# First attention of a two-layer gated block: heads in two halves of the array, queries stacked in lots, a later zero fill and a new order of each pair of steps

## The reference, cut to what matters

```python
x = x + jnp.tanh(g_xattn[0]) * _L0_xattn_ref(_layernorm(x), ctx, Wq, bq, Wk, bk, Wv, bv, Wo, bo)

q = jnp.einsum('btd,hdk->bhtk', tgt, Wq) + bq[None, :, None, :]
k = jnp.einsum('bsd,hdk->bhsk', src, Wk) + bk[None, :, None, :]
v = jnp.einsum('bsd,hdk->bhsk', src, Wv) + bv[None, :, None, :]
weights = jax.nn.softmax(jnp.einsum('bhtk,bhsk->bhts', q, k) / sqrt(16), axis=-1)
out = jnp.einsum('bhts,bhsk->bhtk', weights, v)
return h @ Wo + bo          # h: the heads of out side by side
```

## Time and profile before

| | us |
|---|---|
| runs of the kernel before | 961.48, 964.19, 970.35 (median 964.19) |
| the profiled execution's own time | 963.44 |
| its span, from the first to the last instruction | 961.7 |
| TensorE busy over the span | 754.5 (78%) |
| VectorE busy | 619.2 (64%) |
| ScalarE busy | 481.3 (50%) |
| GpSimd busy | 410.3 (43%) |

### The profile page before, as it was taken

The page is one execution under the profiler, slowest core; times in us unless marked ns, Lnnn a source line. Parts: engine busy times, 40 slices in busy tenths (PEclk is TensorE's granted clock), DMA queues, the critical chain, the costliest instruction groups (busy, mean ns, idle before and its releaser), DMA issues. The chain is left out here.

```text
span 961.7 us, 20435 instructions
## 1 busy us (share of the span) xinstructions
PE 754.5 (78%) x6519; PEld 573.3 (60%) x6519; DVE 619.2 (64%) x1458; ACT 481.3 (50%) x989; POOL 410.3 (43%) x437
## 2 busy tenths in 40 slices
PE   4679999999977398979888889578777548998830
PEld 2356667667656398978666656467666526665420
DVE  8567677767664669873444444377788436666766
ACT  4736565556544467652333333245655236776632
POOL 4268323233160028881000000586856716746455
PEclk9779999999999669999999999788989868999985
DMA  6447322223170238753222221378532212323233
GB/s 159 114 103 164 92 61 67 56 64 77 30 243 9 90 88 274 236 186 114 72 66 67 68 70 48 103 192 206 162 107 67 63 53 91 115 72 96 83 90 100
DMA packets 84511, 101.50 MB, mean 106 GB/s; under 512 B 16518, under 2 KB 70758, under 8 KB 84422
## 3 DMA queue, kind: packets, MB, share of 16 engines
q1 hardware_dynamic: 69526, 68.42, 25.4%
q0 software_dynamic: 12960, 30.74, 11.4%
q10 hardware_dynamic: 1936, 1.17, 0.5%
HBM read 61.03 MB, written 24.38 MB: 89 GB/s over the span
## 5 line engine op out<-in xcount | busy, mean ns | idle before, releaser
L645 DVE TENSOR_REDUCE a_mx<-ps 112x2 f32<-112x750 f32 x128 | 119.8, 936 | 45.1 <-PE ps L323 38.7
L529 ACT ACTIVATE a_Pf<-ps 125x672 f32<-125x672 f32 x128 | 89.7, 729 | 15.6 <-PE ps L271 14.6
L323 PE MATMUL ps<-a_stkK,a_stkQ 96*112 96x375 bf16 x256 | 68.2, 349 | 20.8 <-DMA a_stkK<-a_KS 10.6
L51 PE MATMUL ps<-f_w2hi,f_hh 128*128 (+1 forms) x292 | 81.3, 278 | 3.1 <-DVE f_hl L1432 3.1
L1430 DVE CAST f_hh<-ps 128x512 bf16<-128x512 f32 x41 | 28.4, 692 | 83.9 <-PE ps L1171 83.9
L51 PE MATMUL ps<-f_w2lo,f_hh 128*128 (+1 forms) x292 | 81.2, 278 | 0.0
L51 PE MATMUL ps<-f_w2hi,f_hl 128*128 (+1 forms) x292 | 81.1, 278 | 0.0
L51 PE MATMUL ps<-f_w1hi,f_xgThi 128*128 x150 | 57.9, 386 | 23.6 <-DVE f_xgTlo L1423 17.7
L1719 POOL MEMSET a_half<- 112x2 f32 x1 | 0.1, 94 | 170.3 <-POOLq L89 170.3
L546 POOL DMA_DIRECT2D a_stkK<-a_KS x96 | 51.2, 540 | 45.7 <-DVE a_KS L612 28.9
L540 POOL TENSOR_TENSOR a_ctxL<-a_ctxF,a_ctxH 128x750 bf16<-128x750 f32 x16 | 25.7, 1604 | 104.7 <-ACT a_ctxH L429 104.7
(11 more groups left out here) (403 smaller groups left out, 2367.9 us busy)
## 6 DMA issues: line engine op xcount, KB each, us to landing
a_raw<-F_w SPq DMA_DIRECT2D x22, 512.0 KB, 5.9
f_xg<-f_xd SPq DMA_DIRECT2D x75, 128.0 KB, 2.2
f_yd<-f_yo SPq DMA_DIRECT2D x75, 128.0 KB, 1.7
f_raw<-F_w SPq DMA_DIRECT2D x14, 512.0 KB, 4.1
a_ctxF<-ctxT SPq DMA_DIRECT2D x16, 375.0 KB, 3.5
a_cR<-ctx SPq DMA_DIRECT2D x16, 375.0 KB
a_cT_first<-ctxT SPq DMA_DIRECT2D x14, 375.0 KB, 4.9
f_xd<-a_zero POOLq DMA_DIRECT2D x1, 5248.0 KB, 20.0
```

The costliest lines, as they stand in the source:

```text
L51: ins = nc.tensor.matmul(out, l, r, start=first and i == 0, stop=last and i == len(steps) - 1)
L323: last = nc.tensor.matmul(psMX[:T, h, :S], stkQ[0:96, bass.ds(n.b, 1), j // JJ, j % JJ, h * T:(h + 1) * T].rearrange("p o q -> p (o q)"), ...
L529: nc.scalar.activation(Pf[:, s % PB], psST[:C, s % 2, :SC, :QW], ACT.Exp).then_inc(exp_done, 1)
L645: nc.vector.reduce_max(mx[:, n.odd, 2 * j:2 * j + 2], psMX[:T, :, :S], AX).then_inc(mx_red, 1)
```

## The change

Everything is in `l0_attention`.

- **Heads in two halves.** `stkQ` and `stkK` hold one head of a pair in partitions 0 to 49 and the other in 64 to 113: 16 rows each of keys high, low, high, then two rows for the maxima. No masks: the zeroed copies, `pair` and `qf` are gone, the factor 1/4 moves into exp's scale, and ACT and DVE write the queries' parts straight to `QS` (8 and 8 instructions). `maxima` is two matmuls of 48 rows and 375 columns, `scores` six of 50 rows and 112 columns, one head's into one bank each.
- **Stacking.** 24 pieces of 16 partitions for a batch's keys, 8 issued by SP and 16 by GpSimd. A placing of maxima is 4 DMAs instead of 2.
- **Queries in lots.** Lot 1 (batches 0 to 3): 24 DMAs, 12 on SP and 12 on GpSimd. Lot 2 (batches 4 to 9): 24 DMAs on GpSimd, 8 in each of slots 0 to 2, behind that slot's key stacking. Lot 3 (batches 10 to 15): 24 on GpSimd, 4 in each of slots 3 to 8, at the same place. TensorE waits for lot 2 at the end of slot 2, for lot 3 at the end of slot 8.
- **Order.** The tasks of batch `b+3` run in slot `b`, those of batches 1 and 2 in the prologue (two places in PSUM in turns). In a step: `maxima`, turn of maxima, `values` (odd s), `scores`, task (even s), `turn_values` (even s). On DVE the reduction comes first in the step, on ACT exp comes ahead of the task.
- **Values** are written to columns 336 to 447 of bank 0, one of the scores' banks: `values` and `scores` of even steps now wait for one another's readers (exp, the copy `oT`).
- **Late zero fill.** GpSimd waits, before the fill, until the maxima of the second half of batch 15 are placed.
- GpSimd's and TensorE's lists are unrolled, with no loop.

```diff
-        stkQ = sb("stkQ", [98, B, KD, JJ, QW], BF16)
-        stkK = sb("stkK", [98, 4, KD, JJ, S], BF16)
+        SIDE, KEYS, DOT = P // 2, 3 * DH, 3 * DH + 2
+        stkQ = sb("stkQ", [P, JJ, B, KD, T], BF16)
+        stkK = sb("stkK", [P, 4, JJ, KD, S], BF16)
+        QS = sb("QS", [P, 2, B, KD, T], BF16)
...
-        psST = k.ps[:, 0:4, :].rearrange("p (u b) (two n) -> p u (b two) n", u=2, two=2)
+        psST = k.ps[:, 0:4, :].rearrange("p (u h) n -> p u h n", u=2)
-        psPV = k.ps[:, 6, 0:T]
+        psPV = k.ps[:, 0, SC * T:(SC + 1) * T]
...
-        PIECES = [(jj, a, part) for a, part in ((0, 0), (1, 1), (2, 0)) for jj in range(JJ)]
-        K_IN = len(PIECES) // 2 * 16
+        PIECES = [(jj, h, a, part) for a, part in ((0, 0), (1, 1), (2, 0)) for jj in range(JJ) for h in range(2)]
+        K_SP, K_POOL = PIECES[0::3], PIECES[1::3] + PIECES[2::3]
+        SP_IN, POOL_IN = 16 * len(K_SP), 16 * len(K_POOL)
+        Q_PIECES = [(jj, h, i, part) for jj in range(JJ) for i, part in ((0, 0), (1, 0), (2, 1)) for h in range(2)]
+        Q_TURN = (GB + B) // 2
...
+        def stack_queries(eng, batches, pieces, stacked):
+            for jj, h, i, part in pieces:
+                eng.dma_start(stkQ[SIDE * h + DH * i:SIDE * h + DH * (i + 1), jj, batches],
+                              QS[2 * DH * jj + DH * h:2 * DH * jj + DH * (h + 1), part, batches]).then_inc(stacked, 16)
...
 # SP
                 def place_maxima(n, half):
                     sp.wait_ge(turn_free, 2 * n.b + half + 1)
-                    for part in range(2):
-                        sp.dma_start(stkQ[96 + part:97 + part, bass.ds(n.b, 1), half].rearrange("o b j (h q) -> o (b j h) q", q=T),
-                                     cneg[:, n.odd, half, part, :]).then_inc(c_in[half][n.odd], 16)
+                    for h in range(2):
+                        for part in range(2):
+                            row = SIDE * h + KEYS + part
+                            sp.dma_start(stkQ[row:row + 1, :, bass.ds(n.b, 1), half, :].rearrange("o j b q -> o (j b) q"),
+                                         cneg[JJ * h:JJ * (h + 1), n.odd, half, part, :]).then_inc(c_in[half][n.odd], 16)
...
 # TensorE
                     for c in range(SC):
-                        last = nc.tensor.matmul(psST[:C, j % 2, c, :QW],
-                                                stkK[:, b.slot, j // JJ, j % JJ, c * C:(c + 1) * C],
-                                                stkQ[:, bass.ds(b.b, 1), j // JJ, j % JJ, :].rearrange("p o q -> p (o q)"),
-                                                start=True, stop=True)
+                        for h in range(2):
+                            side = slice(SIDE * h, SIDE * h + DOT)
+                            last = nc.tensor.matmul(psST[:C, j % 2, h, c * T:(c + 1) * T],
+                                                    stkK[side, b.slot, j % JJ, j // JJ, c * C:(c + 1) * C],
+                                                    stkQ[side, j % JJ, bass.ds(b.b, 1), j // JJ, :].rearrange("p o q -> p (o q)"),
+                                                    start=True, stop=True)
...
-                def emit(p, b, n, w, x, l):
+                def emit(p, b, n, ws, x, l):
                     for s in range(NJ):
...
                         if n is not None:
                             maxima(n, s)
                         if b is not None and s == 0:
                             turn_maxima(b, 1)
+                        row, g = (p, 3) if s == 1 else (b, s // 2 - 1)
+                        if row is not None and s % 2 == 1:
+                            values(row, g, p.b * NJ + NJ if b is None else b.b * NJ + s)
+                        if b is not None:
+                            scores(b, s)
                         if n is not None and s == 4:
                             turn_maxima(n, 0)
-                        if w is not None and s % 2 == 0:
-                            (keys if s < 4 else vals)(w, s // 2 % 2)
-                        if b is not None:
-                            scores(b, s)
-                        row, g = (p, 3) if s == 1 else (b, s // 2 - 1)
-                        if row is not None and s % 2 == 1:
-                            values(row, g)
+                        w, t = task_at(ws, s)
+                        if w is not None:
+                            (keys if t < 2 else vals)(w, t % 2)
+                        row, g = (p, 2 + s // 2) if s < 4 else (b, s // 2 - 2)
+                        if row is not None and s % 2 == 0:
...
+                            turn_values(row, g)
+                    if n is not None and n.b in (GB - 1, Q_TURN - 1):
+                        pe.wait_ge(rest_q, 16 * len(Q_PIECES) * (1 if n.b == GB - 1 else 2))
...
 # GpSimd
+                def emit(p, b, n, ws, x, l):
+                    for r in range(2):
+                        for row in x[r:r + 1]:
+                            low_context(row)
+                        for w in ws[r:r + 1]:
+                            stack_keys(w)
+                    if b is not None and b.b < 3:
+                        if b.b == 0:
+                            pool.wait_ge(q_lo, KD * NG)
+                        stack_queries(pool, slice(GB, Q_TURN), Q_PIECES[b.b::3], rest_q)
+                    elif b is not None and b.b < Q_TURN - 1:
+                        stack_queries(pool, slice(Q_TURN, B), Q_PIECES[b.b - 3::Q_TURN - 4], rest_q)
...
+                last = ring(B - 1)
+                pool.wait_ge(c_in[1][last.odd], last.half * 64 + 64)
                 pool.dma_start(xd.rearrange("(n p) d -> p n d", p=P),
                                zero[:].unsqueeze(1).broadcast_to([P, NBLK, D])).then_inc(k.filled, 16)
```

More of the change, by code:

```diff
@@ L363, in _ @@
                 turn_tokens(2)
+                keys(ring(0), 1)
                 queries(1, 0)
@@ L674, in emit @@
                             minus_maxima(n, 0)
-                        if w is not None and s in (1, 3):
-                            low_keys(w, s // 2)
+                        w, t = task_at(ws, s if len(ws) == 2 else s - 1)
+                        if w is not None and t < 2:
+                            low_keys(w, t)
+                        row, g = (p, 2 + s // 2) if s < 4 else (b, s // 2 - 2)
+                        if row is not None and s % 2 == 1:
+                            finish(row, g)
                 run(dve, emit)
```

268 lines of the change are left out of this document (127 added, 141 removed).

## The result

The changed kernel takes 984.21 us (median of four runs, 981.80 to 988.67), the kernel before 965.23 in the same sitting (four runs, 961.48 to 970.35): ratio 1.0198 [1.0135, 1.0262], some 19 us slower. Forecast: 978, range 954 to 992. The profiled execution took 988.67, its span is 986.9; that of before was 961.7.

The account below looks back on a forecast made before the run. TensorE's ordered list was taken to bound the attention loop. Slot 15 at 287.6 against 289.71, projection 10.9 us later and a cold start of 4 gave +14.9 on 963.4: 978 us, range 954 to 992.

Parts of the forecast that it names:

- The start: Before the loop: less masking lets keys stack sooner, first maxima at 39.8 instead of 45.48, 5.7 us won.
- Part 3, GpSimd's queue: GpSimd's DMA issues, 0.54 us each, make lots 2 and 3 late: TensorE stalls of 13.6 and 6.7 us.
- the cooling: Behind the two stalls: TensorE at half clock loses 4 us after the first and 3 after the second.
- Part 1, slots of 13.7: Attention loop: limits of TensorE, DVE and SP give 13.7 us a slot, range 13.0 to 15.9.
- rival D: Loop matmuls: the halves don't run side by side, slots take 15.0 us, total 992; 8 % chance.
- three limits at 13.0 to 13.8: Loop slot: TensorE 13.2, DVE 13.0 and SP's round 13.8 us, taken together as 13.7 a slot.
- two slots of 12.2: Slots 13 and 14, without tasks or fill: DVE's chain of 11.8 sets 12.2 us each, against 31.1 for both before.
- 5.65 + 20.0 + 0.3 = 26.0: Attention's end: release, fill and its wait start the projection 26.0 us after the last turn, against 13.0 before.
- The cold start of the projection, 4: Output projection: TensorE, idle ten microseconds, starts at half clock and loses 4 us, bounds 0 and 6.
- A (deadlines met): GpSimd's queue: it issues the lots in time, 27.3 us of stalls and cooling fall away, 951; 16 % chance.
- B (the fill isn't in the way): Attention's end: the fill lands sooner or the barrier doesn't hold TensorE, 964, no change; 10 % chance.
- C: Loop: shorter slots, TensorE at 12 and DVE at 13.0 set them, 971 or 966; 12 % chance.

Follow-up runs that it names:

- all mended together: Changed kernel with lots ahead of keys, SP's keys in fours, fill's wait in the projection's Block, no GpSimd drain, unused products in slots 13 to 15: 946.35 us, 0.9736.
- The lots-first kernel: Changed kernel with query lots 2 and 3 issued ahead of each slot's subtraction and key stacking on GpSimd, a semaphore per lot: ratio 1.0059.
- extra products: Changed kernel with six more 375-column matmuls over 128 rows, results unused, in each even step of slots 13 to 15: ratio 1.0126.
- the last kernel: Changed kernel with lots first, SP's keys in fours, fill's wait moved, no drain, bias additions ahead of that wait, no unused products: 947.48 us, 0.9809.

## Why the prediction was right or wrong

**Slower by some 15 us, for two stalls and the fill: right** in sign and place; 984.2 lies 6 above the 978. The profiled execution, the slowest of the four, lies 10.7 above: by the table -6.5 up to slot 3, +2.6 over the ten slots, +8.1 over slots 13 and 14, +6.3 to the projection, the rest rounding. So the total is nearer than its terms: the stalls, 10.2 us in this execution, are half of the 20.3 forecast, and two costs at the end that the sum did not have, the half clock and the drain, make up for it. That these errors go against one another is luck.

**The start: right.** First maxima at 38.30 (39.8 forecast), the gain 7.2 instead of 5.7, because an issue was cheaper than its price in the sum.

**Part 3, GpSimd's queue: right in mechanism, the step "an issue of GpSimd costs 0.536 us ... the floor stays for smaller pieces" was mis-sized.** Sixteen pieces take 7.66, 0.48 each. Over the 104 pieces to lot 2 that is 6.2 us less; the landing is 1.9 instead of 2.9 (1.0), the first pieces start at 45.29 instead of 47.3 (2.0), and GpSimd's short gaps give some 2.4 back: together 6.8, as the wait ends at 105.46 instead of 112.3. The range of 0.50 to 0.55 was too narrow below: the floor of one shape had been taken for that of another. The second (3.00, not 6.7) has the same 20 pieces at the lower price and the shorter landing in it, some 1.7 of the 3.7; that gives 5.0, which is what four of the six kernels with this code show (4.61 to 5.03), while this execution and one other have 3.00 and 2.94. The lots-first kernel shows the cause: neither stall is there. Of the cooling, 4 and 3 in the sum, its slots show less: slots 3 and 4 are 1.4 and slot 9 is 1.5 shorter there than in the changed kernel. The signs put the second stall "at about 219 us"; the sum's own terms, 112.5 and six slots of 13.7 with 4 behind the first stall, put the end of slot 8 at 199, and it stands at 196.5 to 199.5.

**Part 1, slots of 13.7: right for slots that nothing disturbs** (13.58 to 14.14 in the changed kernel; 137.8 us for ten of them with all mended together, where the sum had 137), and the maxima's halves do run side by side, so rival D fell. The timeline of the changed kernel has the single gains:
```profile
145.33 0.37 PE L357 MATMUL ps<-a_stkK,a_stkQ 48*112 48x375 bf16 x2
145.63 0.78 PE L313 MATMUL ps<-a_Pf,a_V 125*32 125x112 f32 x24
146.34 0.38 PE L301 MATMUL ps<-a_stkQ,a_stkK 50*125 50x112 bf16 x6
146.74 0.37 PE L357 MATMUL ps<-a_stkK,a_stkQ 48*112 48x375 bf16 x2
146.94 0.33 PE L301 MATMUL ps<-a_stkQ,a_stkK 50*125 50x112 bf16 x6
```
With scores behind them the maxima take 0.20 us, as the sum had it, with values behind them 0.30, against 0.36. The scores take 0.36 to 0.40 up to the next maxima, against 0.39, where 0.1 was taken off. But no switch of mode can be seen as a gap, and the list comes to 85.55 / 91.0 x 13.75 = 12.9 us a slot in the mended kernel, beside 13.2. (The upper bound of 15.9 does not follow from its own terms: a saving of nothing, scores at 0.5 and switches of 0.2 give 14.45 + 0.9 + 1.6 = 16.9.) Missed was what a chain of 13.8 against a slot of 13.7 does: SP's round, worked out as one of "three limits at 13.0 to 13.8", makes TensorE wait 0.90 us or more in six of the slots, and three of these waits also cool it. In this kernel three near limits in different queues gave more than the largest of them. The ten slots took 153.3 instead of 150.7 although the second stall was 3.7 shorter.

**Part 4, the step "two slots of 12.2": wrong.** They took 32.5 together, not 24.4. VectorE's chain was worked out at full clock, but the same step takes away the tasks, the only wide, long matmuls of a slot, and the granted clock falls to 0.50. With extra products the slots take 13.35. Even at full clock 12.2 is not reached, here or in the kernel before without a fill beside it (13.88 in its slot 14); what sets these 13.4 to 13.9 us is open. The kernel before could not warn of the half clock: its slot without tasks keeps 1.00, and the 0.90 of the earlier trace rows is behind the 2.38 us wait (1.00 over 273 to 281, 0.77 and 0.80 over the next two stretches of 4).

**Part 4, the barrier: right that the late fill holds it, wrong in the step "5.65 + 20.0 + 0.3 = 26.0".** Release 4.86, landing 19.7, and then not 0.3 but 7.8: GpSimd arrives last, and its drain comes on top. In the trace of before the 0.3 was the way of a Block whose GpSimd had been done long ago; the price stood in it all the same, as the drain of 7.50 us from 290.1, hidden behind VectorE. The fill took 19.7 to 20.7 us in every run, alone or not. The Trainium skill, page "DMA: Bandwidth & Descriptors", section "Anatomy of one DMA — SWDGE (gpsimd) path", makes it an estimated 14.3 us, and the traces do not agree.

**The cold start of the projection, 4: right as far as it can be seen** (662.8 less 659.0 is 3.8). From its first transposes to those of the next stage it is 30.2 us (324.10 to 354.29) against 27.2 (302.72 to 329.89), with the clock at 0.50 over the first 8. But from the projection's start to the span's end the kernels in which 8 us or more of idle TensorE stand ahead of it range from 662.7 to 668.2, so a single pair of executions does not fix the 4 to within 2.

**Rivals.** A (deadlines met) fell, but more than half of its price of 27.3 was real: the lots-first kernel, which meets them, wins some 16 us between slot 2 and slot 15. (With B together its 951 less 9.8 and 4 is 937, not 935.) It remained slower than before, as the late fill has its own price. B (the fill isn't in the way) fell by the late fill put into the kernel before: it alone costs the 19 us. C fell: no slot of the loop came under 13.4 us at full clock.

## What to carry to other kernels

A transfer that is put late to keep it out of the way of others must not be what a barrier waits for: move its wait to where its data are needed, and let the engine that issues it do its other work first. When an engine's idle time is filled with DMA issues, add up its queue against each deadline and put the pieces with the nearest deadline first; the same pieces in another order were worth some 16 us here. Look for the drain of an engine at the end of a Block in the trace before the change: a price that is hidden now is paid when that engine comes last. Price every slot of a pipeline at the clock that it will have: here the slots without tasks ran at half clock with matmuls of 48 and 50 rows and at full clock with those of 96 and 98, and products whose result nobody reads paid 9.5 us.

## What was not expected of the hardware

- The end of a Block waits for GpSimd's drain: a row of 7.33 or 7.50 us in most of the traces, 10.10 and 10.27 in two. It is paid in full when GpSimd arrives last (7.8 us from the fill's landing to the projection with it, 0.4 without), and unseen when it arrives early.
- GpSimd's DMA issue costs 0.484 us for 16 partitions of 1500 bytes, against 0.536 for 32; the first of these was not in the trace of before.
- Matmuls of 48 rows in the two halves of the array take 0.37 us a pair, in the same half 0.52.
- Half clock with hardly any idle time ahead: in the last kernel TensorE is 82% busy over 237 to 264 (22.18 of 27) and has a granted clock of 0.54; with extra products it is 96% busy, at 1.00 (25.83 of 27). The kernel before with the late fill, without tasks and without extra products, is 72% busy over 274 to 288 (10.12 of 14) and has 1.00: its maxima and scores are matmuls of 96 and 98 rows, those of the last kernel of 48 and 50.
